# Diagonal sums of a correlation with two row halves laid side by side and added by VectorE before one product, where two products ran

## What is computed

```python
qf = jnp.fft.rfft(qt); kf = jnp.fft.rfft(kt)      # q, k, v projected, over the positions
c = qf.real * kf.real + 1j * -(qf.imag * kf.imag)
corr = jnp.fft.irfft(c, n=Lq)
mean_value = jnp.mean(corr, axis=(1, 2))          # over heads and channels: one value per delay
weights, delay = jax.lax.top_k(mean_value, 15)
out = sum_i softmax(weights)[i] * v shifted by delay[i];  x = x + out @ Wo + bo
...
x = x + shared_expert(LN(x)) + the 4 of 16 routed experts that the router picks per row
```

## Time and profile before

| | us |
|---|---|
| three runs | 997.3, 999.38, 1002.05 |
| median | 999.38 |
| the profiled execution | 996.96 |
| its span | 995.1 |

### The profile page before, as it was taken

One profiled execution on the slowest core, in us unless ns is written; L12 is line 12 of the kernel. 1 busy time (PEld: TensorE's weight loads), 2 busy tenths in 40 slices (PEclk: granted clock), 3 DMA queues, 4 the chain that ended last, 5 costly groups with the idle time before them and its releaser, 6 DMA issues.

```text
span 995.1 us, 21034 instructions
## 1 busy us (share of the span) xinstructions
PE 983.5 (99%) x6750; PEld 601.8 (60%) x6750; DVE 655.4 (66%) x1506; ACT 380.2 (38%) x776; POOL 473.6 (48%) x540
## 2 busy tenths in 40 slices
PE   9999999999999999989999999999999999999998
PEld 7776644444444445557777778777777544444443
DVE  4977788874498898965555555555555476676766
ACT  3646454343545333324444444444444311111111
POOL 0725412131145477654445444444543376666672
PEclk9999999999999999999999999999999999999999
DMA  9735867868562711558889988889988578999675
GB/s 348 259 126 196 295 193 233 233 192 237 175 180 96 222 64 64 127 147 248 251 248 239 256 242 249 242 249 233 261 250 230 169 238 260 313 260 307 187 226 177
DMA packets 175483, 216.93 MB, mean 218 GB/s; under 512 B 101096, under 2 KB 112232, under 8 KB 174376
## 3 DMA queue, kind: packets, MB, share of 16 engines
q1 hardware_dynamic: 151640, 136.95, 46.8%
q0 software_dynamic: 23760, 78.79, 26.8%
HBM read 123.67 MB, written 69.22 MB: 194 GB/s over the span
## 4 chain that ended last, share of the span: by engine, by line
PE 81%; DVE 9%; DMA 4%; issue 3%; ACT 2%; SPq 0%; POOL 0%; DVEq 0%; ACTq 0%; POOLq 0%
PE bank L1068 19%; PE bank L941 13%; PE bank L1131 13%; PE bank L1092 9%; PE bank L957 7%; PE bank L1144 6%; PE bank L1051 5%; PE bank L716 2%; PE bank L1082 2%; PE bank L793 1%; DMA arena<-in_x 1%; DMA arena<-xr_dram 1%; PE bank L696 1%; DVE arena L1855 1%; DVE arena L1622 1%
## 5 line engine op out<-in xcount | busy, mean ns | idle before, releaser
L1068 PE MATMUL bank<-arena 128*128 x1716 | 211.0, 273 | 0.9 <-issue 0.7
L941 PE MATMUL bank<-arena 128*128 128x512 f16 x888 | 202.3, 379 | 0.5 <-DVE arena L1616 0.2
L1068 PEld LDWEIGHTS bank<-arena 128*128 128x128 f16 x1716 | 163.0, 98 | 26.1 <-issue 1.4
L2139 POOL DMA_INDIRECT arena<-y_dram,arena x128 | 135.7, 1060 | 77.9 <-issue 28.9
L2082 POOL DMA_INDIRECT arena<-xr_dram,arena x143 | 139.6, 976 | 59.4 <-issue 48.2
L941 PEld LDWEIGHTS bank<-arena 128*128 128x128 f16 x888 | 87.2, 99 | 100.9 <-DVE arena L1616 0.7
L1131 PE MATMUL bank<-arena 128*128 128x512 f16 x648 | 144.1, 379 | 0.6 <-DMA arena<-xr_dram 0.6
L1092 PE MATMUL bank<-arena 128*128 x429 | 115.4, 378 | 0.5 <-ACT arena L1401 0.5
L1884 DVE SCALAR_TENSOR_TENSOR arena<-bank,arena 128x128 f32<-128x128 f32 x143 | 41.7, 292 | 109.5 <-ACT arena L1390 108.7
L1338 ACT ACTIVATE arena<-arena 128x512 f16<-128x512 f32 x64 | 40.3, 629 | 184.4 <-DVE arena L1616 104.5
L1951 DVE SCALAR_TENSOR_TENSOR arena<-arena 128x512 f32<-128x512 f32 x128 | 95.3, 749 | 23.1 <-DMA arena<-y_dram,arena 20.5
(11 more groups left out here) (227 smaller groups left out, 1318.9 us busy)
## 6 DMA issues: line engine op xcount, KB each, us to landing
y_dram<-arena SPq DMA_DIRECT2D x143, 256.0 KB
arena<-in_x SPq DMA_DIRECT2D x8, 1024.0 KB, 12.0
xr_dram<-arena SPq DMA_DIRECT2D x16, 512.0 KB, 3.9
x_dram<-arena SPq DMA_DIRECT2D x8, 1024.0 KB, 5.6
arena<-in_gu_w SPq DMA_DIRECT2D x16, 512.0 KB, 3.5
out<-arena SPq DMA_DIRECT2D x32, 256.0 KB, 3.8
arena<-x_dram SPq DMA_DIRECT2D x5, 1024.0 KB, 6.0
arena<-in_gu_w POOLq DMA_DIRECT2D x8, 512.0 KB, 4.7
```

The lines of the kernel that those rows point to most:

```text
L941: last = mm(bank[half][:, :], (gu_hi_s, gu_lo_s)[wp][:, c, at:at + H], xt[:, xv * KC + kc, :], start=(n == 0), stop=(n == 3 * KC - 1))
L1068: last = mm(gate_up_bank(s, s)[:, 0:2 * H], rows[:, xv * KC + kc, :], only((gu_hi_r, gu_lo_r)[wp], e, slice(kc * 2 * H, (kc + 1) * 2 * H)) ...
L2139: pool.indirect_dma_start(out=ybuf[n % RING][:, e, :], out_offset=None, in_=y_dram[:, :], in_offset=bass.IndirectOffsetOnAxis(ap=row_of[:, ...
```

## The change

The skewed copies now put row q and row q + 64 side by side: partitions 0 to 63 of `skew_near` hold rows 0 to 63 of the first direction, partitions 64 to 127 rows 0 to 63 of the second; `skew_far` holds the rows 64 higher of both. VectorE adds `skew_far` to `skew_near` (`fold_part`), and one product per tile sums the 64 partitions of each direction, with −1 for the lower half in its second column. The bytes and the length of the copied rows stay as they were. For batch 0, where the two buffers lie together, one copy fills both; for batch 1 each copy becomes two. New waits on `s_fold` stand on TensorE (five steps), and on VectorE the waits for the copies that TensorE had. The bias additions of block 4 are split and put later, and the router's preparation goes behind `vo_low(0)`.

```diff
-SUM_AT = {(0, 0, 10): 1, (0, 0, 11): 2, **{(0, 1, n): i + 3 for i, n in enumerate((0, 1, 3, 4, 6, 7, 9, 10))},
-          (1, 0, 11): 0, **{(1, 1, n): n + 11 for n in range(NA - 11)}}
+SUM_AT = {**{(0, 1, n): n - 8 for n in range(9, 12)}, **{(1, 0, n): n + 4 for n in range(7)},
+          (1, 0, 10): 0, (1, 0, 11): 11, **{(1, 1, n): n + 12 for n in range(NA - 12)}}
+FOLD = P // 2
...
         def skewed(b, start, pitch, first, end):
-            return bass.AP(pt_dram, b * P * PTW + start + first, [[pitch, P], [1, end - first]])
+            return bass.AP(pt_dram, b * P * PTW + start + first, [[pitch, FOLD], [FOLD * pitch, 2], [1, end - first]])
...
+                    for v, dst in enumerate((skew_near[1], skew_far[1])):
+                        sp.dma_start(dst[0:FOLD, EARLY - M:L], skewed_half(1, 2 * M - 1, PTW - 1, EARLY - M, L, v)
+                                     ).then_inc(s_sk2[1], 16)
+                        sp.dma_start(dst[FOLD:P, EARLY:L], skewed_half(1, 1, PTW + 1, EARLY, L, v)).then_inc(s_sk2[1], 16)
+                        sp.dma_start(dst[FOLD:P, 0:M], skewed_half(1, 1, PTW + 1, 0, M, v)).then_inc(s_sk2[1], 16)
...
-                mm(dst, skew_c[b][:, a * P:a * P + P], c_sb[:, C_ONES + 2 - SUM_W:C_ONES + 2], start=True, stop=False)
-                return mm(dst, skew_d[b][:, a * P:a * P + P], c_sb[:, C_ONES + 4 - SUM_W:C_ONES + 4], start=False, stop=True)
+                return mm(dst, skew_near[b][:, a * P:a * P + P], c_sb[:, C_ONES + 4 - SUM_W:C_ONES + 4],
+                          start=True, stop=True)
...
-                    if g == half == 0 and n == 10:
-                        pe.wait_ge(s_sk[1], 32)
+                    if g == 0 and half == 1 and n == 9:
+                        pe.wait_ge(s_fold, 4)
                         pe.wait_ge(s_pt_sb, 7)
-                    if g == 1 and half == 0 and n == 11:
-                        pe.wait_ge(s_sk2[1], 48)
+                    if g == 1 and half == 0 and n == 10:
+                        pe.wait_ge(s_fold, 5)
...
+            def fold_part(b, lo, hi):
+                near = skew_near[b][:, lo:hi]
+                return V.tensor_tensor(near, near, skew_far[b][:, lo:hi], ALU.add)
+            def fold_late(b):
+                dve.wait_ge(s_sk2[b], 96 if b else 48)
+                fold_part(b, 0, M)
+                fold_part(b, EARLY - M, L).then_inc(s_fold, 1)
...
+                if g == 0:
+                    fold_late(1)
                 dve.wait_ge(s_shh, g + 1)
                 V.tensor_tensor(s_hb[:, g % 2, 1, :], s_h, s_hb[:, g % 2, 0, :], ALU.subtract).then_inc(s_shl, 1)
...
             x1_moments(1)
+            dve.wait_ge(s_sk[1], 64)
+            fold_part(1, M, EARLY - M).then_inc(s_fold, 1)
             shared_weights_lo(1)
...
-            for q in range(5):
+            for q in range(HALF):
                 add_bo(q)
+            pool.wait_ge(s_ev_sb, 3)
+            add_bo(4, (0, 1, 2))
...
                 shared_weights_in(n)
+            add_bo(4, (3,))
             add_bo(5)
```

98 lines of the change are left out of this document (54 added, 44 removed).

## The result

The changed kernel takes 1015.73 us (median of 6 runs, 1009.96 to 1021.43) where the kernel before takes 999.18 beside it (997.3 to 1002.65, 6 runs). The ratio is 1.0154, with a 95% interval from 1.0125 to 1.0184: slower by 1.5%, where no change was forecast.

A forecast was written before the change was run, and what follows sets the result against it. The prediction took TensorE as the bound, busy 983.5 of 995.1 us. Batch 0's gain of 1.9 us and batch 1's loss of 1.9 summed to no change, 999.4 us on the median, range 995.0 to 1003.6.

The forecast's parts named there:

- The products: TensorE, both batches: 32 fewer products save 3.5 us at each batch, 7.0 us if no wait comes.
- Batch 0's wait: TensorE waits 2.3 us for VectorE's late folds before the last six sums; batch 0 still gains 1.9 us.
- The late copy, issued at 47.2, lands 3.0 later, at 50.2: Batch 0's late skewed copy takes 3.0 us to land, so the last two folds end at 52.3.
- The rival with half of the partitions: Copies into 64 partitions take twice as long: batch 1 loses 4.8 us, batch 0 gains 1.4, 1002.8 us; chance 0.25.
- From there to the attention the chain through VectorE and the small copies is the old one: Batch 0, from sums to attention: the old distance stays, so attention starts at 75.6 instead of 77.47.
- the gain of 1.9 at batch 0: Batch 0: the sums end at 53.8, 1.9 us earlier than before, and the attention follows at 75.6.
- Batch 1: Its saved products go into waits for VectorE and copies; the stage behind its sums comes later, a loss of 1.9 us.
- The wait of 1.8 in the first chunk: Shared expert's chunk 0, batch 1: TensorE loses 1.8 us waiting for the fold that ends at 106.9.
- What was moved: Router preparation and three bias additions cost nothing; one more ahead of block 5's delays GpSimd and batch 1's copies 1.2 us.
- GpSimd against VectorE: Rival at batch 0: the two engines hold each other up, 0.6 us lost instead of 1.9 won, 1001.9 us; chance 0.1.

The follow-up runs named there:

- e10_batch0_corr: e9_inter_corr with batch 1 as in the kernel before (wide copies, two products per tile, no additions of VectorE); 1000.51 us, ratio 0.9997.
- e3_inter: The changed kernel with the first direction's rows copied into the even partitions and the second's into the odd ones; 1016.58 us, ratio 1.0114.
- e2_before_narrow: The kernel before with only the changed kernel's narrow copies: 64 products, no folds, bias additions where they were; 1025.55 us, ratio 1.0218.
- e9_inter_corr: e3_inter with block 4's correlation in TensorE's wait for batch 0's late folds and all four block 4 bias additions behind the even parts; 1003.70 us, ratio 1.0042.
- e1_wide: The changed kernel with the skewed copies of the kernel before, each direction read into all 128 partitions; 1008.43 us, ratio 1.0076.
- e11_batch0_early: e10_batch0_corr with the first value projection moved behind batch 0's sums; 1001.75 us, ratio 0.9988.
- e6_inter_bias: e3_inter with GpSimd's bias additions in the order of the kernel before, 20 in a row, then block 5; 1012.34 us, ratio 1.0120.

## Why the prediction was wrong

- **The products.** Right. Six sums, six products now, take 1.42 us in e10_batch0_corr at a clock of 1.00 (12 records, 0.24 a product; 1.3 was taken). So some 3.5 us less work for TensorE at batch 0 is there; in e10_batch0_corr 2.5 us of it are seen as more idle time ahead of the attention.
- **Batch 0's wait.** The steps on VectorE and GpSimd were near, the landings were not. The folds were priced as waiting for GpSimd (second until 46.9, last until 52.3) and e3_inter, whose copies reach all partitions, has 47.1 and 53.6. In the changed kernel they end at 49.77 and 55.76, behind landings. The failed step is "The late copy, issued at 47.2, lands 3.0 later, at 50.2": it was issued at 50.2 and landed at 54.7, since each copy delays the write behind it, and that write the next copies. The forecast took this step from the wide copy's row, and so left the narrow width out at batch 0 altogether; e2_before_narrow, which has only the narrow copies of the change, issues the same copy at 49.7.
- **The rival with half of the partitions** was the right mechanism at a wrong size. It gave batch 0 half a us and batch 1 2.9 over the forecast, 3.4 in all; between e3_inter and the changed kernel it is 3.8 and 4.7, 8.5 in all, the clock included. It had the transfer doubled and, at batch 1, 2.0 us passed on to one write, but at batch 0 not the chain of write, copy, write, copy, in which every landing counts. The Trainium skill (SBUF — State Buffer, section on the DMA port swizzle) gives 196 GB/s for 1 MiB into partitions 0 to 63 and 328 into all. The trace is near to that, with 205 in the stretch of the late copies and 302 in that of before. Worked out from the map that the Trainium skill has in the same section, every second partition reaches all of the ports. e3_inter, with 282 GB/s from 48 to 50 us, agrees. The chance of 0.25 was too low for a rule that only equal bytes and row lengths spoke against.
- **What stands behind a wait.** The second failed step, missing from every case: "From there to the attention the chain through VectorE and the small copies is the old one". The prediction sized the waits and let TensorE go on at its old pace. At 0.50 the same six sums take 2.77 us (the changed kernel at 55.81) where they take 1.42 at 1.00 (e10_batch0_corr). e9_inter_corr against e3_inter puts the wait of 3.0 and the slow stretch behind it together at 3.0 us of the first mark; with the wait covered and the clock at 1.00, the attention is at 77.0, not at the predicted 75.6.
- **Where the gain of 1.9 at batch 0 was to come from.** The prediction let the attention follow the sums at the old distance; they were to end at 53.8. Sums that early need late folds by 52.3, and with copies that reach all partitions the last two start at 52.55 in e3_inter, behind a landing, and at 51.16 in e1_wide, where they take 2.08 us beside GpSimd's last additions and end at 53.24. In e9_inter_corr, e10_batch0_corr and e11_batch0_early, 0.1 to 0.5 us are gained there.
- **Batch 1.** A loss of 1.9 was predicted, 7.6 came. With the copies spread it is 2.9 (e3_inter), and with batch 1's folds taken away 0.5 (e10_batch0_corr). The wait of 1.8 in the first chunk that was predicted is 1.80 in e3_inter; that the loss through the folds, 2.0, is near the 1.9 predicted is in part luck, since the clock fell in e9_inter_corr and not in e3_inter. The 4.7 between e3_inter and the changed kernel are 3.0 in the start of the late folds, counted from the attention (41.2 against 38.2), and 1.7 behind it, where the clock is 0.50 from 128 to 131. Less the 6.3 of batch 0, the changed kernel issues its last copy at 112.7 and starts these folds at 118.6, where 109.4 and 114.6 were predicted; e3_inter, less its 2.5, has 112.1 and 115.6. So the late issue is for the most part not the width: the six issues take 0.5 to 0.6 us each, and one 1.4 to 1.6, where 0.43 was taken, and the write ahead of them lands later. What the width adds is seen behind the last issue: the folds start 5.9 us after it in the changed kernel and 3.5 in e3_inter.
- **What was moved.** The router's preparation ran from 79.98 on, ahead of the attention, and no wait of TensorE ends there: nothing, as predicted. The bias additions moved behind the even parts cost nothing, as predicted, and they are worth 2.8 us to the late folds (e6_inter_bias). The 16 that stayed took 21.23 us for the 20.3 predicted.
- **GpSimd against VectorE**, the third rival, has a small part in the changed kernel, where the late folds do not meet the additions. The prediction's reading that GpSimd hardly waits for VectorE came from a row without folds. Beside the four folds of e6_inter_bias, 2.5 us by themselves at the prediction's prices, the 20 additions take 1.76 us more than in the earlier trace rows, and the two late folds lose 2.1: each does wait for the other. The changed kernel's 16 end at 52.13 for 50.9 predicted.
